# GpSimd writes the blanks of the attention's score stacks, and the clearing of the FFN slots starts a sequence later in smaller pieces

## The chip, the cores and the metric

The kernel runs on one core of one Trainium2 chip. The metric is the device time of one execution in microseconds, from the median of several runs. The core has TensorE (PE in the profile; its weight loads are PEld), VectorE (DVE), ScalarE (ACT), GpSimd (POOL) and SyncE (SP), each with its own instruction stream. They meet at semaphores. In this part of the kernel all transfers are issued by SP, from one stream, in program order.

## The reference, cut to what matters

Four layers follow each other on 16 sequences of 512 tokens with 256 channels: a first attention, a mixture-of-experts FFN, a second (chunked, linear) attention, and the FFN again. The change lies in the first attention and in what that stage prepares for the FFN.

```python
def _attend(q, k, v, mask):
    scores = jnp.einsum('bhqd,bhkd->bhqk', q, k) * HEAD_DIM ** (-0.5)
    scores = jnp.where(mask[None, None], -jnp.inf, scores)
    w = jax.nn.softmax(scores, axis=-1)
    return jnp.einsum('bhqk,bhkd->bhqd', w, v)
...
x = x + attention_a(layernorm(x), w_qkv, b_qkv, w_out, b_out)   # 16 heads of 16 channels
x = x + ffn(layernorm(x), ...)                                  # top 4 of 16 experts
x = x + attention_b(layernorm(x), ...)
x = x + ffn(layernorm(x), ...)
```

Four of the 16 heads are causal over the whole sequence ("global"), twelve see a window of 64 keys ("local").

## The kernel before, in words

`phase_a` computes the first attention. It runs iterations s = -1 to 16. Iteration s does the *core* of sequence s (scores, exponentials, masks, context), the *front* of sequence s + 1 (layernorm, transposes, q, k, v, the rows of maxima), and the *tail* of sequence s - 1 (output projection, store). Each iteration has NU = 20 units u of scores. In every engine's program the work of front, core and tail is put at fixed units (tables such as `TAIL_AT`, `MASK_AT`, `slot_front`), so the order on each engine is written out by hand. Iteration -1 has a front only, iteration 0 no tail.

The scores are one matmul over 97 rows. The operands are *stacks*: `qs` [128, 16 heads, 512] and `ks` [128, 8 pairs, 512] hold, in rows 0 to 95, the high and low parts of q and k, three products in one contraction. Row 96 (`ONES`) of `ks` is all ones and row 96 of `qs` holds the negated maximum of each query, so the matmul subtracts it. A key pair's stack is read with one head's rows of `qs`; the rows of the other head of the pair must be zero. These zeros in `qs` and the ones in `ks` are the *blanks*. They are written once, at the start, by VectorE (two memsets ahead of its iterations), and SP waits for both (`dve_ready`) before the first `spill`.

SP builds the stacks through HBM: `spill(s, t)` writes the parts of half t of the heads to the scratch `turned`, `stack(s, t)` reads them back in another layout (nine transfers), and `m_rows(s, g)` copies the maxima, g = 0 for the global heads and g = 1 for the local ones. Score units 0 to 7 are the global heads and need `m_rows(s, 0)`; units 8 to 19 are the local ones and need `m_rows(s, 1)`, too.

SP's order in iteration s is: load of x for s + 2; `stack(s, 1)`; `m_rows(s, 1)`; store of sequence s - 1, and a wait for its landing; `spill(s+1, 0)`, `spill(s+1, 1)`, `stack(s+1, 0)`, `m_rows(s+1, 0)`, and `clear(s+1)`.

`clear(i)` belongs to the FFN. The tokens of the FFN are scattered into `slots` tensors in HBM, which must be zero. `clear(i)` writes a part of them from a tile of zeros, 2560 KB each, 16 times. With i = 0 it also writes the last, smaller tensor `slots[-1]` whole, in one transfer of 6144 KB (`FEW` = 6144 rows of 1 KB). At the end of the stage SP waits for all clears (`cleared`).

At the start, in iteration -1: SP loads x of sequence 0, then the weights and biases, then x of sequence 1. VectorE writes the blanks and then computes the statistics of sequence 0 (L549). ScalarE computes a logarithm and an exponential for the inverse deviation and then, at `WEIGHTS_SLOT`, waits for the weights, scales them (L521) and casts their high parts; VectorE subtracts to make the low parts (L667, L668). ScalarE then waits for these before it casts the high part of the transposed x (L454), and q and k follow (L461). GpSimd makes constants (L416 to L439), waits for the weights and adds the bias for the residual (L405).

Of the kernel before, what the change touches and what calls it, by code (L numbers as in the profile page):

```python
# [5 lines left out]
P = 128  # L6
F32 = mybir.dt.float32
# [7 lines left out]
H = 256  # L15
# [77 lines left out]
FEW = STEPS1[1] * STEP * P  # L93
# [8 lines left out]
ONES = 3 * PAIR  # L102
# [47 lines left out]
def phase_a(nc, x_in, x_out, slots, turned, w_qkv, b_qkv, w_out, b_out, nseq):  # L150
# [37 lines left out]
    with ExitStack() as ctx:  # L188
# [3 lines left out]
        def sem(name):  # L192
            return ctx.enter_context(nc.semaphore("a_" + name))
# [23 lines left out]
        ks = sb("ks", [P, PAIRS, SEQ], F32R)  # L217
        qs = sb("qs", [P, HEADS, SEQ], F32R)
# [11 lines left out]
        zeros = sb("zeros", [P, 4 * H])  # L230
# [6 lines left out]
        w_loaded, w_ready = sem("w_loaded"), sem("w_ready")  # L237
        w_high = sem("w_high")
        dve_ready = sem("dve_ready")
        x_loaded = sem("x_loaded")  # L240
        res_ready = sem("res_ready")
        ln_stat = sem("ln_stat")
# [37 lines left out]
        NSTAT = TB + 10  # L280
        W_DMAS = 16 * (4 + 2 * QT)
        SPILL, STACK = 16 * 4, 16 * 9
        mt_at = [FRONT.index(("mT", g)) for g in range(2)]

        with nc.Block() as block:
# [6 lines left out]
            @block.sync  # L292
            def _(sp):
                def load(s, par):
                    rows = seq_rows(sp, x_in, s)
                    read, loaded = in_register(sp, ev(s - 2, 1, 0)), in_register(sp, 16 * s)
                    at_least(sp, ln_done, read)
                    at_least(sp, res_ready, read)
                    at_least(sp, x_loaded, loaded)
                    sp.dma_start(xin[:, par], rows).then_inc(x_loaded, 16)  # L300

                def m_rows(s, g):
                    src, h0, h1 = (mTg, 0, GLOBAL) if g == 0 else (mTl, GLOBAL, HEADS)
                    last = 2 * t_last[0] + 1 if g == 0 else 2 * NU - 1
                    made = in_register(sp, ev(s, NF, mt_at[g]))
                    used = in_register(sp, ev(s - 1, 2 * NU, last))
                    copied = in_register(sp, 16 * (2 * s + g))
                    at_least(sp, f_dve, made)
                    at_least(sp, s_done, used)
                    at_least(sp, m_row, copied)  # L310
                    sp.dma_start(qs[ONES:ONES + 1, h0:h1, :].bitcast(F32), src[:].bitcast(F32)).then_inc(m_row, 16)

                def spill(s, t):
                    at_least(sp, stacked[t], STACK * s)
                    at_least(sp, f_dve, ev(s, NF, at["k", t]))
                    for i, part in enumerate((kh, kl, qh, ql)):
                        sp.dma_start(turned[i][t * P:(t + 1) * P, :], part[:, t, :].bitcast(F32)).then_inc(spilled[t], 16)

                def stack(s, t):
                    at_least(sp, s_done, ev(s - 1, 2 * NU, 2 * t_last[2 * t + 1] + 1))  # L320
                    at_least(sp, spilled[t], SPILL * (s + 1))
                    for i, (k, q) in enumerate(((0, 2), (0, 3), (1, 2))):
                        r = i * PAIR
                        sp.dma_start(ks[r:r + PAIR, t * PT:(t + 1) * PT, :].bitcast(F32),
                                     turned[k][t * P:(t + 1) * P, :].rearrange("(a c) n -> c a n", c=PAIR)
                                     ).then_inc(stacked[t], 16)
                        for j in range(2):
                            sp.dma_start(qs[r + j * DH:r + (j + 1) * DH, t * HT + j:(t + 1) * HT:2, :].bitcast(F32),
                                         turned[q][t * P:(t + 1) * P, :].rearrange("(a j d) n -> j d a n", j=2, d=DH)[j]
                                         ).then_inc(stacked[t], 16)  # L330

                def clear(i):
                    if i == 0:
                        sp.wait_ge(zeroed, 1)
                    q = SLOTS // BATCH
                    sp.dma_start(slots[i // BATCH][i % BATCH * q:(i % BATCH + 1) * q, :].rearrange("(p r) h -> p (r h)", p=P),
                                 zeros[:].unsqueeze(1).to_broadcast([P, q // P // 4, 4 * H])).then_inc(cleared, 16)
                    if i == 0:
                        sp.dma_start(slots[-1].rearrange("(p r) h -> p (r h)", p=P),
                                     zeros[:].unsqueeze(1).to_broadcast([P, FEW // P // 4, 4 * H])).then_inc(cleared, 16)  # L340

                def body(s, par, tail, core, front):
                    if tail:

                        rows = seq_rows(sp, x_out, s - 1)
                        summed, stored = in_register(sp, ev(s - 1, NTAIL, NTAIL - 1)), in_register(sp, 16 * s)
                    if not isinstance(s, int) or 2 <= s + 2 < nseq:
                        load(s + 2, par)
                    if core:
                        stack(s, 1)  # L350
                        m_rows(s, 1)
                    if tail:
                        at_least(sp, t_dve, summed)
                        sp.dma_start(rows, xres[:, 1 - par]).then_inc(x_stored, 16)
                        at_least(sp, x_stored, stored)
                    if front:
                        if s < 0:
                            sp.wait_ge(dve_ready, 2)
                        spill(s + 1, 0)
                        spill(s + 1, 1)  # L360
                        stack(s + 1, 0)
                        m_rows(s + 1, 0)
                        clear(s + 1)

                sp.dma_start(xin[:, 0], seq_rows(sp, x_in, 0)).then_inc(x_loaded, 16)
                sp.dma_start(wraw[:], w_qkv.rearrange("(k p) n -> p k n", p=P)).then_inc(w_loaded, 16)
                sp.dma_start(oraw[:], w_out.rearrange("(k p) n -> p k n", p=P)).then_inc(w_loaded, 16)
                for b, c0 in ((bq, 0), (bk, H)):
                    for t in range(QT):
                        sp.dma_start(b[:, t:t + 1], b_qkv[c0 + t * P:c0 + (t + 1) * P].rearrange("(p o) -> p o", o=1)  # L370
                                     ).then_inc(w_loaded, 16)
                sp.dma_start(bv[:], row_broadcast(b_qkv[2 * H:3 * H])).then_inc(w_loaded, 16)
                sp.dma_start(bo[:], row_broadcast(b_out)).then_inc(w_loaded, 16)
                sp.wait_ge(x_loaded, 16)
                sp.dma_start(xin[:, 1], seq_rows(sp, x_in, 1)).then_inc(x_loaded, 16)
                for s in range(-1, nseq + 1):
                    body(s, s % 2, s >= 1, 0 <= s < nseq, s < nseq - 1)
                sp.wait_ge(x_stored, 16 * nseq)
                sp.wait_ge(cleared, 16 * (nseq + 1))

            @block.gpsimd
            def _(pool):
# [55 lines left out]
                nc.gpsimd.tensor_copy(identb[:], ident[:]).then_inc(w_ready, 1)  # L438
                nc.gpsimd.memset(vv[:, :, :, :, DH:VW], 1.0).then_inc(w_ready, 1)  # L439
                pool.wait_ge(w_ready, 12)  # L440
                pool.wait_ge(w_loaded, W_DMAS)
                iterations(pool, body)

            @block.scalar
            def _(act):
# [56 lines left out]
                def body(s, par, tail, core, front):  # L502
                    for u in range(NU):
# [15 lines left out]
                        if isinstance(s, int) and s == -1 and u == WEIGHTS_SLOT:  # L519
                            act.wait_ge(w_loaded, W_DMAS)  # L520
                            nc.scalar.activation(wraw[:, :, 0:H], wraw[:, :, 0:H], ACT.Copy, scale=DH ** -0.5).then_inc(w_scaled, 1)  # L521
                            nc.scalar.activation(bq[:], bq[:], ACT.Copy, scale=DH ** -0.5).then_inc(w_scaled, 1)
                            act.wait_ge(w_scaled, 2)
                            nc.scalar.copy(wh[:], wraw[:]).then_inc(w_high, 1)
                            nc.scalar.copy(woh[:], oraw[:]).then_inc(w_high, 1)
                            act.wait_ge(dve_ready, 4)
                        if core:
                            exps(s, u)
                            for t in range(3):
# [15 lines left out]
            def _(dve):  # L545
# [129 lines left out]
                                if u == K_AT[t]:  # L675
                                    half_k(s + 1, t)

                nc.vector.memset(qs[0:ONES].bitcast(F32), 0.0).then_inc(dve_ready, 1)
                nc.vector.memset(ks[ONES:ONES + 1].bitcast(F32), 1.0).then_inc(dve_ready, 1)
                dve.wait_ge(dve_ready, 2)  # L680
                iterations(dve, body)

            @block.tensor
            def _(pe):
# [6 lines left out]
                def front_use(s, par, i):  # L691
# [8 lines left out]
                            ins = pe.transpose(dst[:, b * P:(b + 1) * P], xn[:, b, k * P:(k + 1) * P], ident[:])  # L700
                    elif kind in ("q", "k"):
                        if isinstance(s, int) and s == 0 and i == at["q", 0]:
                            pe.wait_ge(dve_ready, 4)
                        at_least(pe, f_dve, ev(s, NF, at["T", 1]))
                        w = slice(k * P, (k + 1) * P) if kind == "q" else slice(H + k * P, H + (k + 1) * P)
                        for c in range(KT):
# [2206 lines left out]
```

## Time and profile before

| what | value |
|---|---|
| median of 3 runs | 2695.92 us (2694.72 to 2711.29) |
| profiled execution, its own time | 2692.55 us |
| its span | 2690.8 us |
| TensorE busy | 2336.5 us, 87% |
| VectorE busy | 1825.3 us, 68% |
| ScalarE busy | 1486.1 us, 55% |
| GpSimd busy | 1371.2 us, 51% |
| HBM traffic | 202 GB/s over the span |

The span is that of the profiled execution, from the first to the last instruction. The first attention takes about the first 807 us of it. A timeline row gives the start, the duration, the engine, the line in the kernel, the operation, and the tiles written and read; in brackets stands how long the engine was idle before it and what ended that. "SPq" rows are the issues of transfers by SP: their duration is that of issuing, not of the transfer. "x4" is four such instructions merged into one row.

### The profile page before, as it was taken

The page shows a single profiled execution, that of the slowest core. Times are in us where ns is not written, and L with a number is a line of the kernel's source. Part 1 is how long each engine was busy: PE and PEld are TensorE (multiplying, and loading weights), DVE is VectorE, ACT ScalarE, POOL GpSimd, SP SyncE. Part 2 cuts the span into 40 slices and gives each one's busy share as a digit, 9 for nine tenths or more (in the row PEclk, how much of TensorE's full clock was granted, in tenths as well). Part 3 has the DMA queues.
Part 4 walks back from the last instruction along what each step waited for, and adds up shares of the span by engine and source line. Part 5 has one row for each costly group of instructions (what it writes and reads, how often), then busy time and mean ns, then how long its engine had stood idle before and what let it go on. Part 6 is the DMA issues. An engine that isn't in the chain of part 4 may idle for free. (4 is left out here: it accounts for less than half of the span.)

```text
span 2690.8 us, 50440 instructions
## 1 busy us (share of the span) xinstructions
PE 2336.5 (87%) x15632; PEld 1877.2 (70%) x15632; DVE 1825.3 (68%) x4784; ACT 1486.1 (55%) x2987; POOL 1371.2 (51%) x1591
## 2 busy tenths in 40 slices
PE   5799999999976889889995999999889399999983
PEld 3566666666754678779984777777677397888861
DVE  7577777767636877665565788888776554666654
ACT  3576767676642446457773454435444276666640
POOL 1353434444341735447443544777776165554566
PEclk9899999999987899989996999999899699999996
DMA  6887786868644657559884333445443598888874
GB/s 205 176 211 191 195 207 185 213 179 215 161 120 159 215 192 245 201 200 335 306 306 145 95 110 119 152 149 162 137 149 131 186 315 283 294 307 295 307 249 149
DMA packets 255835, 548.41 MB, mean 204 GB/s; under 512 B 33490, under 2 KB 125652, under 8 KB 254548
## 3 DMA queue, kind: packets, MB, share of 16 engines
q1 hardware_dynamic: 206420, 410.90, 50.4%
q0 software_dynamic: 49152, 134.28, 15.0%
q8 instruction: 131, 2.15, 0.3%
q14 instruction: 132, 1.08, 0.1%
HBM read 267.71 MB, written 276.82 MB: 202 GB/s over the span
## 5 line engine op out<-in xcount | busy, mean ns | idle before, releaser
L389 POOL TENSOR_SCALAR_AFFINE_SELECT a_pt<-a_pt 128x512 f32<-128x512 f32 (+1 forms) x320 | 174.3, 545 | 438.1 <-ACT a_pt L485 437.4
L1026 POOL DMA_INDIRECT slots<-f_xn,k_picks x256 | 261.9, 1023 | 243.2 <-PE f_Z L1534 89.7
L2615 POOL DMA_INDIRECT f_yg<-made,k_picks x256 | 254.0, 992 | 174.0 <-PE f_Z L2808 102.6
L485 ACT ACTIVATE a_pt<-a_S 128x384 f32<-128x384 f32 (+3 forms) x640 | 255.0, 456 | 147.0 <-PE a_S L744 145.7
L1754 POOL DMA_INDIRECT k_yg<-made,k_picks x224 | 224.2, 1001 | 128.5 <-issue 61.1
L620 DVE TENSOR_REDUCE a_mx<-a_FB 128x2 f32<-128x384 f32 (+4 forms) x512 | 271.0, 589 | 17.8 <-PE a_FB L724 17.8
L1764 POOL DMA_INDIRECT slots<-b_staged,k_picks x192 | 196.3, 1022 | 81.1 <-issue 57.3
L722 PE MATMUL a_FB<-a_kb,a_qb 128*128 128x192 bf16 (+4 forms) x1024 | 173.6, 257 | 32.5 <-DVE a_mx L620 24.3
L744 PE MATMUL a_S<-a_qs,a_ks 97*128 97x384 f32 (+3 forms) x640 | 185.2, 370 | 18.9 <-DMA a_qs<-a_mTl 16.2
L467 ACT ACTIVATE a_qb<-a_qh,a_headmask 128x512 bf16<-128x512 f32 x256 | 182.0, 729 | 0.0
L2740 DVE SCALAR_TENSOR_TENSOR f_cb<-f_yg,k_wall,f_cb 128x256 f32<-128x256 f32 x256 | 124.2, 485 | 83.8 <-DMA f_yg<-made,k_picks 76.6
L2660 ACT COPY f_wt<-f_wexp 128x512 f32 x240 | 147.1, 620 | 56.8 <-issue 30.4
L1141 ACT COPY f_wt<-f_wexp 128x512 f32 x252 | 155.6, 619 | 38.1 <-issue 32.6
L1534 PE MATMUL f_Z<-f_xe,f_wt 128*128 128x128 f32 x1344 | 168.8, 280 | 0.0
L1534 PEld LDWEIGHTS f_Z<-f_xe,f_wt 128*128 128x128 f32 x1344 | 161.8, 197 | 0.1
L1544 PE MATMUL f_Y<-f_wt,f_ge 128*128 128x256 f32 x672 | 160.0, 381 | 0.9 <-DVE f_ye L1411 0.9
L2818 PE MATMUL f_Y<-f_wt,f_ge 128*128 128x256 f32 x640 | 153.3, 383 | 5.2 <-DVE f_ye L2731 5.2
L2808 PE MATMUL f_Z<-f_xe,f_wt 128*128 128x128 f32 x1280 | 156.1, 275 | 0.0
L722 PEld LDWEIGHTS a_FB<-a_kb,a_qb 128*128 128x128 bf16 x1024 | 77.8, 98 | 107.8 <-DVE a_mx L620 71.0
L2808 PEld LDWEIGHTS f_Z<-f_xe,f_wt 128*128 128x128 f32 x1280 | 149.3, 192 | 0.2
L2367 PE MATMUL b_Y<-b_wo,b_o 128*128 128x256 f32 x512 | 127.7, 394 | 17.2 <-DVE b_o L2196 17.1
L1405 DVE TENSOR_TENSOR f_ge<-f_r 128x512 f32<-128x512 f32 x84 | 58.2, 693 | 121.8 <-ACT f_r L1154 121.8
(395 smaller groups left out, 6140.5 us busy)
## 6 DMA issues: line engine op xcount, KB each, us to landing
f_xg<-slots SPq DMA_DIRECT2D x164, 512.0 KB, 6.1
made<-f_ye SPq DMA_DIRECT2D x164, 512.0 KB, 3.8
slots<-a_zeros SPq DMA_DIRECT2D x16, 2560.0 KB, 11.1
a_ks<-turned SPq DMA_DIRECT2D x96, 256.0 KB, 7.7
a_qs<-turned SPq DMA_DIRECT2D x192, 128.0 KB, 8.2
a_xin<-in_x SPq DMA_DIRECT2D x16, 512.0 KB, 14.2
turned<-a_kh SPq DMA_DIRECT2D x32, 256.0 KB, 2.6
turned<-a_kl SPq DMA_DIRECT2D x32, 256.0 KB, 2.9
```

Of the source, the lines that this page charges most:

```text
L389: ins = nc.gpsimd.affine_select(out=v[:, :, 0:P], in_=v[:, :, 0:P], compare_op=ALU.is_ge, fill=0.0, base=0, pattern=[[0, nh], [1, P]], cha ...
L467: nc.scalar.activation(qb16[:, h, :], qh[:, t, :].bitcast(F32), ACT.Copy, scale=headmask[:, h % HT:h % HT + 1]).then_inc(q_masked, 1)
L485: nc.scalar.activation(pt[:, u % 4, b * w:(b + 1) * w], S[:, s_bank[2 * u + b], 0:w], ACT.Exp).then_inc(e_done, 1)
L620: nc.vector.tensor_reduce(mx[:, heads[0]:heads[0] + nh, qb], src[:, 0:nh * n].rearrange("p (h c) -> p h c", c=n), AX.X, ALU.max).then_inc( ...
L722: pe.matmul(o[:, j], qb16[:, h, qb * P:(qb + 1) * P], kb16[:, h // HT, k0:k0 + n], start=(j == 0), stop=False, skip_group_check=True)
L744: ins = pe.matmul(S[:, s_bank[i], 0:nh * n], ks[0:ONES + 1, h // 2, kb * P:(kb + 1) * P], qs[0:ONES + 1, h:h + nh, kb * P:kb * P + n], sta ...
L1026: nc.gpsimd.indirect_dma_start(out=slots[GROUP1[s]][:, :], out_offset=bass.IndirectOffsetOnAxis(ap=picks[:, i:i + 1], axis=0), in_=xn[:, s ...
L1534: ins = pe.matmul(Z[:, b * P:(b + 1) * P], wt[:, v % WT, b, k * P:(k + 1) * P], xe[:, v % 2, k, b * P:(b + 1) * P], start=(k == 0), stop=( ...
L1754: nc.gpsimd.indirect_dma_start(out=yg[:, b, k, :], out_offset=None, in_=made[GROUP1[s]][:, :], in_offset=bass.IndirectOffsetOnAxis(ap=rout ...
L1764: nc.gpsimd.indirect_dma_start(out=slots[s // BATCH][:, :], out_offset=bass.IndirectOffsetOnAxis(ap=picks[:, j:j + 1], axis=0), in_=staged ...
L2615: nc.gpsimd.indirect_dma_start(out=yg[:, b, k, :], out_offset=None, in_=made[s // BATCH][:, :], in_offset=bass.IndirectOffsetOnAxis(ap=pic ...
L2808: ins = pe.matmul(Z[:, b * P:(b + 1) * P], wt[:, v % WT, b, k * P:(k + 1) * P], xe[:, v % 2, k, b * P:(b + 1) * P], start=(k == 0), stop=( ...
```

## The change

VectorE's two memsets of the blanks go. GpSimd does them, behind its constants and ahead of its wait for the weights, on a semaphore of their own (`stack_blank`), for which SP now waits before the first `spill`. The waits on `dve_ready` by ScalarE and TensorE count 2 in place of 4, for the same two subtractions.

`clear` moves from the front to the core: iteration s issues `clear(s)` in place of `clear(s+1)`, at the same place in SP's order, the end of the iteration. The 6144 KB transfer is cut into four of 1536 KB, issued behind `clear(3)`, `clear(7)`, `clear(11)` and `clear(15)`. The last wait counts three transfers more.

```diff
+        stack_blank = sem("stack_blank")
+        CLEAR_PARTS = 4
+        CLEAR_EVERY = nseq // CLEAR_PARTS
+        assert FEW % (CLEAR_PARTS * 4 * P) == 0
...
 def clear(i):
...
-                    if i == 0:
-                        sp.dma_start(slots[-1].rearrange("(p r) h -> p (r h)", p=P),
-                                     zeros[:].unsqueeze(1).to_broadcast([P, FEW // P // 4, 4 * H])).then_inc(cleared, 16)
+                    if i % CLEAR_EVERY == CLEAR_EVERY - 1:
+                        q, j = FEW // CLEAR_PARTS, i // CLEAR_EVERY
+                        sp.dma_start(slots[-1][j * q:(j + 1) * q, :].rearrange("(p r) h -> p (r h)", p=P),
+                                     zeros[:].unsqueeze(1).to_broadcast([P, q // P // 4, 4 * H])).then_inc(cleared, 16)
...
 def body(s, par, tail, core, front):     # SP
...
                     if front:
                         if s < 0:
-                            sp.wait_ge(dve_ready, 2)
+                            sp.wait_ge(stack_blank, 2)
                         spill(s + 1, 0)
                         spill(s + 1, 1)
                         stack(s + 1, 0)
                         m_rows(s + 1, 0)
-                        clear(s + 1)
+                    if core:
+                        clear(s)
...
-                sp.wait_ge(cleared, 16 * (nseq + 1))
+                sp.wait_ge(cleared, 16 * (nseq + CLEAR_PARTS))
...
 # GpSimd
                 pool.wait_ge(w_ready, 12)
+                nc.gpsimd.memset(qs[0:ONES].bitcast(F32), 0.0).then_inc(stack_blank, 1)
+                nc.gpsimd.memset(ks[ONES:ONES + 1].bitcast(F32), 1.0).then_inc(stack_blank, 1)
+                pool.wait_ge(stack_blank, 2)
                 pool.wait_ge(w_loaded, W_DMAS)
...
 # ScalarE
-                            act.wait_ge(dve_ready, 4)
+                            act.wait_ge(dve_ready, 2)
...
 # VectorE
-                nc.vector.memset(qs[0:ONES].bitcast(F32), 0.0).then_inc(dve_ready, 1)
-                nc.vector.memset(ks[ONES:ONES + 1].bitcast(F32), 1.0).then_inc(dve_ready, 1)
-                dve.wait_ge(dve_ready, 2)
...
 # TensorE
-                            pe.wait_ge(dve_ready, 4)
+                            pe.wait_ge(dve_ready, 2)
```

## Rows read from the trace of the kernel before

**Rows 1.** The page: the span and the routine clears among the DMA issues.
```profile
span 2690.8 us, 50440 instructions
...
slots<-a_zeros SPq DMA_DIRECT2D x16, 2560.0 KB, 11.1
```

**Rows 2.** DMA issues of the first 60 us: KB each, us from issue to landing.
```profile
slots<-a_zeros SPq DMA_DIRECT2D x1, 6144.0 KB, 24.8
```

**Rows 3.** Timeline, 0 to 60 us: start, duration, instruction, [idle before <-releaser].
```profile
2.58 6.88 DVE L678 MEMSET a_qs<- 96x8192 f32 x1 [2.58 <-issue]
...
4.32 1.80 POOL L439 MEMSET a_vv<- 128x2048 f32 x1
...
5.24 0.43 SPq L375 DMA_DIRECT2D a_xin<-in_x  x1
8.88 2.35 POOL L405 TENSOR_TENSOR a_xres<-a_xin,a_bo 128x1024 f32<-128x1024 f32 x1 [2.76 <-DMA a_bo<-in_b_out]
10.37 3.47 DVE L679 MEMSET a_ks<- 1x4096 f32 x1 [0.91 <-DMA a_xin<-in_x]
13.88 1.40 DVE L549 BATCH_NORM_STATS2 a_stats<-a_xin 128x6 f32<-128x256 f32 x4
...
16.55 0.61 ACT L521 ACTIVATE a_wraw<-a_wraw 128x512 f32<-128x512 f32 x1
...
17.47 1.38 DVE L582 TENSOR_SCALAR a_xn<-a_xin,a_mean,a_rstd 128x256 f32<-128x256 f32 x4
...
21.71 1.07 ACT L454 CAST a_xh<-a_FB 128x512 fp32r<-128x512 f32 x2 [2.43 <-DVE a_wol L668]
...
30.53 0.33 SPq L317 DMA_DIRECT2D turned<-a_kh  x1
```

**Rows 4.** Timeline of the SP queue: its issues in sequences 0 to 3.
```profile
46.06 0.75 SPq L311 DMA_DIRECT2D a_qs<-a_mTg  x1
46.86 0.62 SPq L336 DMA_DIRECT2D slots<-a_zeros  x1
47.52 0.65 SPq L339 DMA_DIRECT2D slots<-a_zeros  x1
48.28 9.21 SPq L300 DMA_DIRECT2D a_xin<-in_x  x1
...
71.84 0.86 SPq L311 DMA_DIRECT2D a_qs<-a_mTl  x1
...
103.91 0.66 SPq L311 DMA_DIRECT2D a_qs<-a_mTg  x1
...
150.64 0.58 SPq L336 DMA_DIRECT2D slots<-a_zeros  x1
...
167.93 0.79 SPq L311 DMA_DIRECT2D a_qs<-a_mTl  x1
...
196.06 0.61 SPq L311 DMA_DIRECT2D a_qs<-a_mTg  x1
```

**Rows 5.** Timeline of VectorE: the negated local maxima of sequence 0.
```profile
57.94 0.67 DVE L627 TENSOR_SCALAR a_mTl<-a_FB 12x512 fp32r<-12x512 f32 x1
```

**Rows 6.** Timeline of TensorE around score unit 8, sequences 0 and 2.
```profile
68.62 0.64 PE L757 MATMUL a_PV<-a_pt,a_vv 128*32 128x256 f32 x8
85.46 1.01 PE L744 MATMUL a_S<-a_qs,a_ks 97*128 97x384 f32 x2 [16.20 <-DMA a_qs<-a_mTl]
...
179.64 0.51 PE L744 MATMUL a_S<-a_qs,a_ks 97*128 97x384 f32 x2
```

**Rows 7.** Timeline of ScalarE: last upper halves of k, sequences 1 and 3.
```profile
68.55 0.69 ACT L461 ACTIVATE a_kh<-a_FB,a_bk 128x512 fp32r<-128x512 f32 x1 [0.70 <-PE a_FB L689]
...
177.46 0.69 ACT L461 ACTIVATE a_kh<-a_FB,a_bk 128x512 fp32r<-128x512 f32 x1 [0.71 <-PE a_FB L689]
```

**Rows 8.** Windows: us, engines' busy time, granted clock, DMA share, GB/s.
```profile
85.00:90.00 5.00, 4.54 (x24) 3.90 (x24) 0.76 (x2) 2.03 (x5) 1.27 (x2) 0.51 0.82 311
```

**Rows 9.** Timeline of the SP queue: the last stores of the attention.
```profile
773.59 30.27 SPq L354 DMA_DIRECT2D x_after_a<-a_xres  x2
```

## The prediction

> **What bounds the kernel now.** I read the page, then the list of waits of the attention, then timelines. The change touches only the first attention, 807 us of a span of 2690.8 us [rows 1]. Two stretches of it matter, the start and sequence 0. From sequence 1 on the iterations repeat: SP issues the global maxima at 103.91 for sequence 1 and at 196.06 for sequence 3 [rows 4], a period of (196.06 - 103.91) / 2 = 46.07 us.
>
> At the start, VectorE is the one that is late [rows 3]. Its blanks take 6.88 and 3.47 us and the statistics of sequence 0 begin at 13.88. The x that they read was in long before: SP waits for it before it issues the load at 5.24. ScalarE scales the weights at 16.55, behind the logarithm and exponential that VectorE's statistics feed. The weights were in at 8.88, when GpSimd, which waits for the same transfers, starts the residual.
>
> In sequence 0, TensorE finishes what goes ahead of score unit 8 at 68.62 + 0.64 = 69.26 and then waits 16.20 us for the rows of local maxima [rows 6]. VectorE had these ready at 57.94 + 0.67 = 58.61 [rows 5], yet SP issues their transfer at 71.84 [rows 4], and they land about 13 us after that. The cause stands in the same rows: at 46.86 and 47.52 SP has issued two clears, 2560 and 6144 KB, and the next issue, at 48.28, already takes 9.21 us. The 6144 KB need 24.8 us to land [rows 2], and the nine stack transfers and the maxima go behind them.
>
> **The start, worked out.** Without the memsets the statistics begin at 5.24 at the latest. From their start to the weights' scaling there are 16.55 - 13.88 = 2.67 us of VectorE and ScalarE [rows 3], so ScalarE is at its wait for the weights by 7.91, and goes on at 8.88. That wait is what binds now: the gain is 16.55 - 8.88 = 7.67 us, not the 10.35 of the memsets. The normalising (L582, 1.38 us) starts 3.59 after the statistics, 8.83, and is done by 10.2; the transposes of TensorE are then done well before ScalarE casts x at 21.71 - 7.67 = 14.04. Everything from there to the maxima of sequence 0 moves by 7.67.
>
> On GpSimd the memsets start at 4.32 + 1.80 = 6.12. Its rate is 1.80 us for 2048 elements [rows 3], 0.88 ns each; so 8192 and 4096 elements cost 7.2 and 3.6 us, done at 16.9. (VectorE's 6.88 us for 8192 is nearly the same rate.) They are needed when SP first spills, 30.53 - 7.67 = 22.86, so 6.0 us of cover are left, and I cost them at nothing. Behind them on GpSimd stands the residual of sequence 0, 2.35 us, then at 19.3; its reader is the tail of sequence 0, after 96 us. If the cover were gone, each microsecond of lateness would be a microsecond of the front.
>
> A rule speaks against this. The row shows four normalisations of 256 elements in 1.38 us [rows 3], about 0.33 us each, 0.78 elements per ns: a rate of one element per cycle or so, and beside GpSimd's residual VectorE's blanks ran on. The Trainium skill ("VectorE: DVE Perf Modes", section "Mode 2×_2P — use both read ports for one tensor"; "SBUF — State Buffer", section "Who interferes with whom") says that such a one-source fp32 operation can take a port that GpSimd shares, as an exclusive lock, so that the second to come waits to the end of the first. By it the normalising would stand behind a memset of 7 us, and the start would gain less. Its two-elements-per-cycle rate is not what the row shows, so the sum leaves it out; it is rival A.
>
> **Sequence 0, worked out.** Without clears, SP issues the load and `stack(0, 1)` at once, and the local maxima when VectorE has them, 58.61 - 7.67 = 50.9. Unit 8 is due at 69.26 - 7.67 = 61.6, 10.7 us later. Before, with 2560 KB in the queue, rows issued at 167.93 were early enough for unit 8 at 179.64, 11.7 us later, with no wait [rows 4, 6]. So the 16.20 us should go whole.
>
> How much is then saved? Two alignments with sequence 2 bound it. By TensorE: from unit 8 to the next global maxima took 103.91 - 85.46 = 18.45 us, against 196.06 - 179.64 = 16.42 in sequence 2 [rows 4, 6]. The 2.03 us more are the clock: after the rest it was granted 0.51 (1.2 GHz) from 85 to 90 us [rows 8], and the pair of score matmuls took 1.01 instead of 0.51. That makes 16.20 + 2.03 = 18.2 us. By ScalarE: the last upper half of k starts at 68.55 in sequence 0, and in sequence 2 the maxima follow 196.06 - 177.46 = 18.60 after it [rows 7]; so they would have come at 87.15 and not at 103.91: 16.8 us. The two differ since sequence 0 has no tail, whose output matmuls sit just ahead of unit 8 in sequence 2; ScalarE, with its exponentials and masked copies, is then the later one. I take 17.0, near the ScalarE end, as it is the one that ends last.
>
> **The moved clears.** 16 issues of 0.6 us stay 16; three more are added, in spots where SP waits afterwards anyway. Four of them now move 4096 KB. The 8704 KB of before landed 47.52 + 24.8 - 46.86 = 25.5 us after the first issue [rows 2, 4], 341 KB per us, so a piece of 1536 KB adds 4.5 us to the queue. Between the clear at 150.64 and unit 8 at 179.64 lie 29.0 us, and the maxima are issued 17.3 after the clear [rows 4, 6]: 11.7 us of room. I cost the pieces at nothing; the far bound, in proportion to the stall, is 16.20 x 1536 / 6144 = 4.05 us for each of three (12.2). The last piece, with the last clear, has no core behind it: it goes out when the store of sequence 14 has landed, some 3 us after 773.59, and the last store follows at 773.59 + 30.27 = 803.86 at the end of that row [rows 9]. The normal clear lands in 11.1 us [rows 1], 4.5 more make 15.6, half of the 27 us there; so the end of the stage sees nothing.
>
> **Sum:** 7.67 + 17.0 = 24.7 us. The profiled execution took 2692.55 us, so 2667.9. The median stands 3.4 above that: 2695.92 - 24.7 = 2671.2, and I predict 2671, which is 0.92% faster. About 1% (27 us) is what a measurement tells from no change; the forecast lies just inside.
>
> **Rivals.**
> A. *The port.* The normalising waits for the first memset (to 13.3) and ends at 14.7; with the transposes (about 2 us) the cast is at 16.8, not 14.04: 21.9 us gained, 2674. If it waits for both, to 16.9, the cast is at 20.4: 18.3 gained, 2678. For it: the rule. Against: the rate in the row. Chance 0.10.
> B. *Half a wait comes back.* Each 1536 KB piece costs its 4.05 us in the iterations behind clears 3, 7 and 11: 12.2 us back, 12.5 gained, 2683. For it: SP's issues do stretch behind clears. Against: the 11.7 us of room. Chance 0.10.
> C. *Slower.* SP's issue stream jams behind 4096 KB as it did behind 8704 (9.21 us for one load). Each of the three iterations then loses as sequence 0 did, 16.20: 48.6 - 24.7 = 24 us slower, 2720. It decides from 24.7 / 3 = 8.2 us a piece. Chance 0.05.
> D. *It does less than it says*: the wait of sequence 0 is that of the nine stack transfers themselves, not of the clears. Then only the start gains: 2688. Against: sequences 1 to 15 have the same nine and no wait. Chance 0.04.
> E. *All of it and more:* TensorE's alignment holds (18.2) and the cold stretch at the start is a little shorter; 26 to 29 us, 2667 to 2670. Chance 0.21.
> The forecast itself, 2669 to 2674: 0.50.
>
> **Range and chances.** 2664 to 2683 holds E, the forecast, A and most of B; it leaves out C, D and the outliers of a median whose runs spread from 2694.72 upwards. Faster by over 1% (below 2669) takes the greater part of E and a little of the forecast's edge: 0.26. Slower by over 1%: C, 0.05. Within 1%: 0.69.
>
> **What would show it.** Right: the statistics of sequence 0 start near 5, the scaling of the weights near 8.9, the first spill near 22.9; no wait at unit 8, which comes near 62; the global maxima of sequence 1 go out near 79.2, the period stays 46.07 throughout. Wrong: normalising later than 9.5 beside a GpSimd memset (A); a wait of TensorE for `a_qs` in sequences 4, 8 and 12, or SP issues of several us there (B, C); a wait at unit 8 in sequence 0 (D); a GpSimd memset that ends after 22.9, or a last clear that lands after the last store.

## The result, and the profile after

The changed kernel takes 2676.2 us (median of 10 runs, 2669.16 to 2692.99) against 2695.32 for the kernel before (10 runs, 2690.09 to 2711.29). The ratio is 0.9929, 95% interval [0.9912, 0.9945]: 19 us less, where 24.7 were forecast. It lies within 1%. The profiled execution of the changed kernel is its slowest run, 2692.99 us with a span of 2691.3, so the two profiles side by side seem to show no gain at all. Three things have to be read apart.

**The start gained nothing.** Timeline of the changed kernel, 0 to 31 us, columns as in [rows 3]:

```profile
4.32 1.80 POOL L445 MEMSET a_vv<- 128x2048 f32 x1
4.70 1.41 DVE L558 BATCH_NORM_STATS2 a_stats<-a_xin 128x6 f32<-128x256 f32 x4 [4.70 <-DMA a_xin<-in_x]
...
6.17 6.92 POOL L447 MEMSET a_qs<- 96x8192 f32 x1
...
6.50 6.62 DVE L568 TENSOR_SCALAR a_mean<-a_mean 128x4 f32<-128x4 f32 x1
6.57 6.55 DVE L569 TENSOR_TENSOR a_yy<-a_yy 128x4 f32<-128x4 f32 x1
6.65 6.48 DVE L570 TENSOR_SCALAR a_var<-a_var 128x4 f32<-128x4 f32 x1
...
13.15 3.51 POOL L448 MEMSET a_ks<- 1x4096 f32 x1
...
13.75 0.61 ACT L530 ACTIVATE a_wraw<-a_wraw 128x512 f32<-128x512 f32 x1
13.87 0.16 DVE L578 TENSOR_TENSOR a_yy<-a_guess 128x4 f32<-128x4 f32 x1 [0.51 <-ACT a_guess L485]
14.07 0.16 DVE L580 TENSOR_TENSOR a_yy<-a_yy,a_var 128x4 f32<-128x4 f32 x1
14.27 2.42 DVE L582 TENSOR_SCALAR a_yy<-a_yy 128x4 f32<-128x4 f32 x1
...
16.74 2.35 POOL L411 TENSOR_TENSOR a_xres<-a_xin,a_bo 128x1024 f32<-128x1024 f32 x1
16.92 3.29 DVE L591 TENSOR_SCALAR a_xn<-a_xin,a_mean,a_rstd 128x256 f32<-128x256 f32 x4
20.13 1.75 DVE L676 TENSOR_TENSOR a_wl<-a_wraw,a_wh 128x1536 fp32r<-128x1536 f32 x1
...
22.51 1.07 ACT L463 CAST a_xh<-a_FB 128x512 fp32r<-128x512 f32 x2 [6.03 <-DVE a_wol L677]
...
30.75 0.33 SPq L321 DMA_DIRECT2D turned<-a_kh  x1
```

The statistics do start at 4.70. But the next tensor_scalar, of 4 elements, takes 6.62 us: it ends when GpSimd's memset ends (6.17 + 6.92 = 13.09). A second one (L582) takes 2.42 and ends with the second memset; the normalising (L591) takes 3.29 instead of 1.38, beside GpSimd's residual. Between them two tensor_tensor (L578, L580) run beside the second memset in their usual 0.16. L569, too, is a tensor_tensor, and shows 6.55: it stands right behind L568 on VectorE and ends with it, so its row does not tell whether it would have stopped alone. And the statistics (L558), which read a single tensor, ran beside GpSimd's memset of `a_vv` in 1.41 us, against 1.40 before.

The stops add up along VectorE's order. The statistics begin 9.2 us earlier than before (4.70 against 13.88). Behind L568 2.8 us of that are left: the weights are scaled at 13.75 against 16.55. Behind L582 0.55 are left (16.92 against 17.47), and behind the normalising VectorE is late: the low parts of the weights begin at 20.13 against 19.32, and the cast of x at 22.51 against 21.71. The first spill is at 30.75, against 30.53 [rows 3]: the 7.67 us are not there.

**The wait in sequence 0 is gone, with what it cost.** SP's queue in the changed kernel, which answers to [rows 4]:

```profile
46.26 0.77 SPq L315 DMA_DIRECT2D a_qs<-a_mTg  x1
47.14 0.40 SPq L304 DMA_DIRECT2D a_xin<-in_x  x1
...
58.84 0.79 SPq L315 DMA_DIRECT2D a_qs<-a_mTl  x1
...
85.84 0.62 SPq L315 DMA_DIRECT2D a_qs<-a_mTg  x1
86.51 0.79 SPq L340 DMA_DIRECT2D slots<-a_zeros  x1
...
133.39 0.62 SPq L315 DMA_DIRECT2D a_qs<-a_mTg  x1
...
181.24 0.63 SPq L315 DMA_DIRECT2D a_qs<-a_mTg  x1
```

And TensorE and ScalarE around unit 8 ([rows 6] and [rows 7]):

```profile
67.41 0.64 PE L763 MATMUL a_PV<-a_pt,a_vv 128*32 128x256 f32 x8
67.97 0.44 PE L750 MATMUL a_S<-a_qs,a_ks 97*128 97x384 f32 x1
```

```profile
67.34 0.69 ACT L470 ACTIVATE a_kh<-a_FB,a_bk 128x512 fp32r<-128x512 f32 x1 [0.70 <-PE a_FB L695]
```

The local maxima go out at 58.84 and unit 8 starts at 67.97, without a wait. From the global maxima of sequence 0 to those of sequence 1 it takes 85.84 - 46.26 = 39.58 us, where it took 103.91 - 46.06 = 57.85: 18.27 less.

**Iterations became longer, in this execution.** The next two steps in the queue's fence are 133.39 - 85.84 = 47.55 and 181.24 - 133.39 = 47.85 us, not 46.07. In 8 of its iterations TensorE's granted clock falls to 0.50 (1.2 GHz) for some 3 to 4 us, each time from 13 to 14 us behind the issue of the global maxima. The windows of the first fall (columns as in [rows 8]):

```profile
98.00:100.00 2.00, 1.11 (x9) 0.60 (x9) 1.97 (x6) 1.12 (x4) 0.81 (x2) 0.91 1.12 147
100.00:102.00 2.00, 2.00 (x10) 1.02 (x12) 1.72 (x7) 0.68 (x2) 0.00 (x0) 0.50 1.08 162
102.00:104.00 2.00, 2.00 (x14) 0.69 (x6) 0.08 (x1) 0.19 (x1) 0.41 (x1) 0.73 1.03 134
```

Ahead of it TensorE has waited twice for VectorE's maxima, and with the fall its next matmuls are long (0.99 against 0.60 for the same pair in sequence 2 of the kernel before, which stood behind the same two waits, 1.07 and 0.89, without a fall):

```profile
97.48 0.34 PE L728 MATMUL a_FB<-a_kb,a_qb 128*128 128x192 bf16 x2 [1.06 <-DVE a_mx L629]
...
99.89 1.01 PE L736 MATMUL a_FB<-a_ident,a_mx 128*12 128x128 f32 x4 [0.89 <-DVE a_mx L629]
100.55 0.99 PE L750 MATMUL a_S<-a_qs,a_ks 97*128 97x384 f32 x2
```

Such an iteration takes 47.5 to 47.9 us, 1.6 more. Eight of them are about 13 us: the FFN's first load is issued at 802.01, against 807.45 before, only 5.4 earlier and not 18. From there to the end this execution took 2691.3 - 802.01 = 1889.3 us against 1883.3, so the rest went there. The experiments show whether the change has a part in that.

### The profile page after: what moved, and what is told of

Its sections match the earlier page's. It is cut to its first block and busy times, and to the rows that moved or that the text cites. A ratio compares the mean times of both kernels' runs of the same rounds, so it can differ in the third digit from the quotient of the medians.

```text
span 2691.3 us, 50441 instructions
## 1 busy us (share of the span) xinstructions
PE 2349.2 (87%) x15632; PEld 1878.3 (70%) x15632; DVE 1827.2 (68%) x4782; ACT 1485.7 (55%) x2987; POOL 1379.8 (51%) x1593
```

## The experiments

All ratios are to the kernel before, run on the same chip in the same session.

### Each half alone

blanks_only: the blanks as in the change, the clears as before. Against the changed kernel (the 6144 KB, whole behind `clear(0)` again, are not shown):

```diff
-                    if core:
-                        clear(s)
+                        clear(s + 1)
```

> Only the blanks move to GpSimd; all clears stay where they were. Theory 'port' (VectorE's tensor_scalar stands still until the GpSimd memset beside it ends, as in the changed kernel): the first spill stays at 30 to 31 us, the wait at unit 8 stays at 16 us, ratio to before 1.000. Rival 'the blanks do save their time, and it was lost later': the same late spill would be seen, but a ratio near 0.997 (7.7 us) if the profiled execution was untypical.

Measured: 1.001 [0.9994, 1.0027], first spill at 31.41, wait at unit 8 17.2 us. This half is worth nothing.

clears_only: the changed kernel, but the two memsets back on VectorE.

> The blanks stay on VectorE; the clears move and are cut as in the change. Theory 'all of the gain is the clears': wait at unit 8 gone, global maxima of sequence 1 issued at 85.6 us, ratio 0.993 (18 us less), the same as the whole change. Rival 'each part gives half': ratio 0.996 to 0.997.

Measured: 0.9933 [0.9909, 0.9958], median 2674.24. That is the whole change's 0.9929. No wait at unit 8. (Sequence 0 took 42.08 and not 39.58 us between the maxima; the granted clock was down from 55 to 62 us in this execution.) The gain is the clears' alone.

### Who stops VectorE

small_blanks cuts GpSimd's memsets in 24 pieces (the waits for them, not shown, count 24):

```diff
-                nc.gpsimd.memset(qs[0:ONES].bitcast(F32), 0.0).then_inc(stack_blank, 1)
-                nc.gpsimd.memset(ks[ONES:ONES + 1].bitcast(F32), 1.0).then_inc(stack_blank, 1)
+                for h in range(HEADS):
+                    nc.gpsimd.memset(qs[0:ONES, h, :].bitcast(F32), 0.0).then_inc(stack_blank, 1)
+                for i in range(PAIRS):
+                    nc.gpsimd.memset(ks[ONES:ONES + 1, i, :].bitcast(F32), 1.0).then_inc(stack_blank, 1)
```

> The changed kernel with GpSimd's two memsets cut into 16 and 8 pieces of 512 elements (about 0.45 us each). Theory 'port, held for the whole instruction': VectorE gets in between the pieces, waits of at most 0.5 us for each of some 8 one-source operations; weights scaled by 9 to 11 us, first spill at 23 to 26 us (blanks are ready near 17 to 18), 5 to 7 us less than the changed kernel, ratio to before 0.990 to 0.991. Rival 'GpSimd and VectorE share bandwidth, or the first waits have another cause': spill stays near 30.7, ratio 0.993.

Measured: 0.99 [0.9876, 0.9925], median 2667.74. Its timeline of VectorE:

```profile
6.57 0.61 DVE L570 TENSOR_SCALAR a_mean<-a_mean 128x4 f32<-128x4 f32 x1
...
8.33 0.28 DVE L584 TENSOR_SCALAR a_yy<-a_yy 128x4 f32<-128x4 f32 x1
...
8.85 2.24 DVE L593 TENSOR_SCALAR a_xn<-a_xin,a_mean,a_rstd 128x256 f32<-128x256 f32 x4
```

The same instruction that took 6.62 us takes 0.61, about one piece. The weights are scaled at 9.24 and the first spill is at 22.77.

two_sources leaves the memsets whole, and gives the layernorm's one-source instructions a second tensor operand (two of the four are shown):

```diff
-  nc.vector.tensor_scalar(mean[:], mean[:], 0.5, None, ALU.mult)
+  nc.vector.scalar_tensor_tensor(out=mean[:], in0=mean[:], scalar=-0.5, in1=mean[:], op0=ALU.mult, op1=ALU.add)
...
-  nc.vector.tensor_scalar(xn[:, b, :], xin[:, par, b, :], mean[:, b:b + 1], rstd[:, b:b + 1], ALU.subtract, ALU.mult)
+  nc.vector.scalar_tensor_tensor(out=xn[:, b, :], in0=xin[:, par, b, :], scalar=mean[:, b:b + 1],
+                                 in1=rstd[:, b:b + 1].to_broadcast([P, H]), op0=ALU.subtract, op1=ALU.mult)
```

> The changed kernel, GpSimd's memsets whole, but the one-source tensor_scalar instructions of the layernorm (three of 128x4 and the four of the normalising) written as scalar_tensor_tensor with a second tensor operand (small constant tiles, or the inverse deviation broadcast). Theory 'only one-source operations wait for a GpSimd memset': none of them lasts over 0.5 us at the start, weights scaled at 8.9 to 9.3 us, first spill at 22.5 to 23.5 us, ratio to before 0.990. Rival 'any VectorE instruction beside a long GpSimd memset can wait': some of them still last 2 to 6.6 us and the spill stays near 30.7, ratio 0.993.

Measured: 0.9862 [0.9834, 0.989], median 2662.36. Its timeline:

```profile
6.19 6.92 POOL L449 MEMSET a_qs<- 96x8192 f32 x1
...
6.61 0.16 DVE L570 SCALAR_TENSOR_TENSOR a_mean<-a_mean 128x4 f32<-128x4 f32 x1
6.69 0.16 DVE L572 TENSOR_TENSOR a_yy<-a_yy 128x4 f32<-128x4 f32 x1
...
8.42 1.67 DVE L596 SCALAR_TENSOR_TENSOR a_xn<-a_xin,a_mean,a_rstd 128x256 f32<-128x256 f32 x4
8.76 0.63 ACT L532 ACTIVATE a_wraw<-a_wraw 128x512 f32<-128x512 f32 x1 [1.17 <-DMA a_bo<-in_b_out]
```

Beside the same memset of 6.92 us nothing of VectorE's stops, and ScalarE now waits for the weights' transfer, as the forecast had it. First spill 23.05. The tensor_tensor behind the first of them (L572, L569 in the changed kernel) takes 0.16 now, so it had only stood in line. So it is the form of VectorE's instruction that decides, and for how long is decided by the length of GpSimd's.

The changed kernel, this version and both edits together, timed side by side on one chip:

> The changed kernel, timed on the same chip as the next two. Both theories: ratio to before 0.993.

> The changed kernel with the two-operand layernorm, timed beside the changed kernel. If its start alone differs (first spill 7.7 us earlier, iterations unchanged): 0.990 to 0.991. If the first measurement (0.986) stands for something more in the later iterations: 0.986 to 0.987 again, and the number of iterations of 47.6 us is smaller than in the changed kernel.

> Two-operand layernorm and GpSimd's blanks in 24 pieces. If nothing of VectorE's waits for GpSimd is left with either edit alone, the second adds nothing: first spill 22.5 to 23.5, the same ratio as the run before it. If waits are left: up to 1 us earlier.

Measured: changed kernel 0.9929 [0.9904, 0.9954], 2674.01 us; two_sources 0.9882 [0.986, 0.9905], 2663.85; both edits 0.9901 [0.9879, 0.9922], 2668.7. The second edit adds nothing to the first. two_sources was measured at 0.9862 and at 0.9882, each inside the other's interval; 0.9862 lies below the interval of both edits, so nothing shows that it is worth more than the second figure. It beats the kernel before clearly, and the changed kernel by some 10 us (2674.01 - 2663.85). In the profiles of these two the first spill is at 22.21 against 30.88, which explains 8.7 of these.

### Which transfer made the wait

big_only: the kernel before, with only the 6144 KB cut in four behind clears 3, 7, 11 and 15; the 2560 KB clears stay a sequence early.

```diff
-                    if i == 0:
-                        sp.dma_start(slots[-1]...)            # 6144 KB
+                    if i % CLEAR_EVERY == CLEAR_EVERY - 1:
+                        sp.dma_start(slots[-1][j * q:(j + 1) * q, :]...)   # 1536 KB
```

> As before, but the 6144 KB transfer is cut in four behind clears 3, 7, 11, 15; the 2560 KB clears stay a sequence early, and the blanks on VectorE. Theory 'the 6144 KB alone makes the wait': no wait at unit 8 of sequence 0, ratio 0.993. Rival 'any clear in sequence 0 delays': a wait of 3 to 8 us stays, ratio 0.995 to 0.998.

Measured: 0.9955 [0.9936, 0.9974], and a wait that is short, but there. SP's queue and TensorE in sequence 0:

```profile
46.34 0.62 SPq L338 DMA_DIRECT2D slots<-a_zeros  x1
...
58.10 0.83 SPq L313 DMA_DIRECT2D a_qs<-a_mTl  x1
```

```profile
66.66 0.64 PE L760 MATMUL a_PV<-a_pt,a_vv 128*32 128x256 f32 x8
70.52 0.61 PE L747 MATMUL a_S<-a_qs,a_ks 97*128 97x384 f32 x2 [3.22 <-DMA a_qs<-a_mTl]
...
763.54 0.79 PE L747 MATMUL a_S<-a_qs,a_ks 97*128 97x384 f32 x3 [1.56 <-DMA a_qs<-a_mTl]
```

So, by this profile, the 6144 KB made some 13 of the 16.20 us, and the routine clear of 2560 KB the last 3.2: the rival said that 3 to 8 us would stay, and a ratio of 0.995 to 0.998. The maxima are issued as soon as VectorE has them, at 58.10, and still come too late. The clear stands 21.0 us ahead of the place of unit 8 here (46.34 to 67.30), and 29.0 us ahead of it in sequence 2 of the kernel before, where the same 2560 KB cost nothing. A second wait, of 1.56 us, stands in sequence 15, behind the last clear and the last piece. In clears_only, where both moved, TensorE never waits for these rows (`a_mTl`). Both parts of the move thus take a wait away. The median is 8.3 us above that of clears_only (2682.53 against 2674.24); the two waits explain 4.8 of these in the profile, the intervals of the two overlap, and this profile had three iterations of 47.6 us: the exact worth of the smaller part is not settled.

whole_at_3: the changed kernel, but the 6144 KB whole, behind `clear(3)`.

> The changed kernel, but the 6144 KB go out whole, behind clear(3). Theory 'the queue delays the maxima by what is in flight, and unit 8 has its place 29 us behind the clear': with 8704 KB in flight the maxima land some 38.6 us behind the clear, so a wait of about 9 to 10 us appears at unit 8 of sequence 4 (near 259 us), ratio 0.996 to 0.997. Rival 'only the place in sequence 0 was the trouble': no wait, ratio 0.993.

Measured: 0.9957 [0.9937, 0.9977], and this on its TensorE, in sequence 4:

```profile
263.16 1.01 PE L749 MATMUL a_S<-a_qs,a_ks 97*128 97x384 f32 x2 [7.81 <-DMA a_qs<-a_mTl]
```

with SP's queue in front of it:

```profile
226.21 0.58 SPq L340 DMA_DIRECT2D slots<-a_zeros  x1
226.83 0.65 SPq L343 DMA_DIRECT2D slots<-a_zeros  x1
227.58 10.68 SPq L304 DMA_DIRECT2D a_xin<-in_x  x1
```

That iteration took 55.45 us. The wait (7.8, not 9 to 10) came back with the 6144 KB, and shorter than in sequence 0: unit 8 was due 29.2 us behind the clear here, and 22.4 us behind it there.

### Whose are the long iterations

before_again and after_again: both kernels unchanged, profiled once more.

> The kernel before, profiled once more. Theory 'the clock falls for some 4 us in some iterations of the attention, and in which is left to each execution, whatever the kernel': here, too, some iterations of about 47.6 us between ones of 46.07, in other places than in the first profile (which had none after sequence 0). Rival 'the falls came with the change': every iteration from sequence 1 on takes 46.07 us.

> The changed kernel, profiled once more. Theory 'left to each execution': first spill at 30.7 us again and no wait at unit 8, but another number than 8 of iterations with a fall of the clock, and the span lower or higher by about 1.6 us for each. Rival 'fixed by the kernel': the same 8 iterations, span near 2691.

Measured: spans 2696.9 and 2678.5 us. The kernel before now had five long iterations after sequence 0 (its first profile none), the changed kernel two (its first profile eight). Over all thirteen profiles, "long" being over 47 us between two global maxima, from sequence 1 on:

| profile | maxima seq. 0 to 1 | long iterations | first load of the FFN | span less that |
|---|---|---|---|---|
| before | 57.85 | 0 | 807.45 | 1883.3 |
| before_again | 58.17 | 5 | 815.54 | 1881.4 |
| blanks_only | 58.52 | 3 | 810.81 | 1888.4 |
| after | 39.58 | 8 | 802.01 | 1889.3 |
| after_again | 41.10 | 2 | 793.71 | 1884.8 |
| after_timed | 39.60 | 0 | 789.56 | 1881.7 |
| clears_only | 42.08 | 0 | 789.73 | 1881.0 |
| big_only | 42.98 | 3 | 798.80 | 1888.4 |
| whole_at_3 | 39.62 | 3, and that of 55.45 | 801.76 | 1882.3 |
| small_blanks | 39.64 | 2 | 780.96 | 1884.8 |
| two_sources | 39.75 | 0 | 780.10 | 1878.6 |
| two_sources_timed | 39.70 | 0 | 780.94 | 1884.6 |
| both | 39.73 | 1 | 782.86 | 1889.3 |

Neither the number of long iterations nor the time of the rest follows the kernel. Where both have none, before and after_timed, the FFN starts 807.45 - 789.56 = 17.9 us earlier, and the spans differ by 2690.8 - 2671.3 = 19.5.

## Why the prediction was right, and where it was not

**The start: wrong.** The step that failed is "the sum leaves it out": I set the normalising's 0.33 us for 256 elements against the rule's double rate, and concluded that the port was not shared. The rate says nothing of that. The instruction was slow by that measure, and still stopped. Rival A had the mechanism, but the wrong place and price: I looked at the large instruction only, while the first to stop was a 4-element one (L568), ahead of the logarithm and so of the weights' scaling, for the rest of a 6.92 us memset; then L582 for the second, and the normalising for the residual. Instead of 21.9 or 18.3 us in all, the start gave -0.2 (30.53 to 30.75). The Trainium skill ("SBUF — State Buffer", section "Who interferes with whom") names tensor_scalar as an operation that can take the pair of ports that GpSimd uses and says that the second one blocks until the first ends, and that an operation with two SBUF inputs stops only for a GpSimd operation that reads. The first half agrees with the traces here: L568 stopped for 6.62 us. Of the second they show one side: beside a memset, which only writes, nothing of two_sources stopped; no row shown here has such an instruction beside a GpSimd operation that reads. What I worked out for a start without that stop was right: with it away, the weights were scaled at 8.76 and the spill was at 23.05, forecast at 8.88 and 22.86. GpSimd's memsets, forecast to end at 16.9, ended at 16.66.

**Sequence 0: right.** 17.0 us forecast, 18.27 in the profile. ScalarE's alignment holds: from its last upper half of k to the next maxima it took 85.84 - 67.34 = 18.50 us, against 18.60 in sequence 2 before. The further 1.4 us lie ahead of it: that part took 67.34 - 46.26 = 21.08 instead of 68.55 - 46.06 = 22.49, since the kernel before had a fall of the clock at 55 to 60 us that this execution had not. That is chance: after_again, with the fall at the same place (56 to 61), took 41.10, which is 57.85 - 41.10 = 16.75 less, and ScalarE's alignment had said 16.8.

**The pieces at nothing: right.** 1536 KB land in 11.4 to 13.8 us; in after_timed the iteration behind clear 3 took 46.27 us, those around it 46.06 and 46.05, and in none of the three profiles of the changed kernel does TensorE wait for the rows of local maxima. The far bound of 4.05 us and rivals B and C are out. whole_at_3 shows that the room I counted with (29 us behind a clear) is real and can be used up: it waits 7.8 us. Rival D, that the stack transfers made the wait, is out by the changed kernel itself, which has the same nine and no wait. What the forecast took as one cause, "two clears", had two parts of unequal size: big_only leaves 3.22 us to the routine clear. Both were moved, so the forecast of no wait held.

**The end of the stage: right.** The last clears go out at 771.49 and 772.12, the last store at 798.62.

**The sum.** -0.2 and 18.3 make 18.1; the timed difference is 19.1 (15 to 24 by the interval). The forecast of 24.7 was too high by 7.9 in the start, less 1.3 that sequence 0 gave more; the range was wide enough by rivals A and B. That the median of 2676.2 lies in it is owed to this width: a third of the forecast gain (7.67 of 24.7 us) never came. What the forecast did not have was the size of one execution's chance: I took "the period stays 46.07" from a profile that happened to have no long iteration.

## What to carry to other kernels

Moving a fill from VectorE to GpSimd is free only if VectorE's instructions beside it are of a form that does not stop for GpSimd; look at the small ones on the critical chain, too, as a long GpSimd instruction holds a 4-element one to its end. Cut the fill in pieces, or give VectorE's instructions two tensor operands. A large background transfer in the same queue as the loads that a step waits for is a matter of bytes in flight against the distance to that step: with 29 us to the step 2560 KB and 4096 KB cost nothing here and 8704 KB a wait of 7.8 us; with 21 to 22 us, 2560 KB cost 3.2 (in the one profile of big_only) and 8704 KB 16.2 us. The one iteration with less distance than the others is the one to look at. And before a change of under 1% is read off two profiles, profile each kernel again: here the same kernel's spans differed by 20 us (2671.3 to 2691.3).

## What the runs showed of the hardware

- VectorE's tensor_scalar of 128x4 fp32 took 6.62 us beside a GpSimd memset of 6.92 us, which only writes; scalar_tensor_tensor and tensor_tensor of the same size took 0.16 beside the same memset, unless they stood behind a stopped tensor_scalar (L569, 6.55 us). The statistics, which read one tensor, ran beside another memset of GpSimd in 1.41 us, as they do alone.
- A transfer of 24 KB that unit 8 needs, issued 11.8 us behind a clear of 2560 KB in the same queue (big_only, 58.10 - 46.34), let TensorE start at 70.52, 12.4 us after its issue.
- TensorE's clock fell to 1.2 GHz for some 4 us in 0 to 8 of 14 iterations of the same code, each time from 13 to 14 us behind the global maxima, where TensorE had just waited some 1.06 and 0.89 us for VectorE (the fall behind the 7.81 us of whole_at_3 left aside). The same waits stand in iterations without a fall (1.07 and 0.89 in sequence 2 of the kernel before). The Trainium skill ("TensorE: Matmul & The Clock Gate", section "Part 1: The HAM clock gate (the "warmup" mystery)") says that the hardware watches activity in a rhythm that does not start with the kernel; that the falls differ between executions of one kernel agrees, but no run here shows the rhythm itself.
- The rest of the kernel, which no edit touched, took 1878.6 to 1889.3 us over thirteen profiles. What makes the difference stays open.
